# A decoder layer on one core: attention weights transposed by row halves, with four smaller moves of work around it

## The chip, the cores and the metric

One Trainium2 chip, one core of it. The metric is device microseconds of one execution of the whole program, as the median of several runs.

## The reference

Sixteen sequences of 128 tokens with 128 features go through one decoder layer, all in float32:

```python
x = layernorm(x + attention(x))            # 16 sequences, 16 heads of 64: Q, K, V, softmax(Q K^T / 8) V, then W_O
x = layernorm(x + cross(x, ctx_1024))      # 16 heads of 64; at each token, the heads attend to one another:
    scores = einsum('bshd,bsgd->bshg', q, k) / 8      # 16 x 16 for each token, softmax over g
    out    = einsum('bshg,bsgd->bshd', softmax(scores), v)   # then reshaped across tokens, then W_o
x = layernorm(x + ffn(x))                  # light: 128 -> 64 -> 128 for all tokens
                                           # heavy: 128 -> 512 -> 128 for the routed ones; 128 are chosen of 128
```

Both feed-forward parts therefore work on all tokens, with RMS normalisation ahead of them and a GELU inside.

## The kernel before

Five instruction streams are written by hand: TensorE (PE), VectorE (DVE), ScalarE (ACT), GpSimd (POOL) and SyncE (SP). They meet only through counting semaphores; nothing is scheduled by a planner, so the order of the code is the order on each engine. There are 16 sequences and 18 steps. Step s handles three sequences at once: the attention scores and softmax of sequence s, the attention output, first normalisation and cross queries of sequence s-1, and the cross output of sequence s-2. Projections of queries and keys are made for four sequences together, so the steps differ by phase, which is s modulo 4. A step of phase 3 projects the first queries of the next four, a step of phase 0 the rest of them, and a step of phase 1 the cross keys; the phase 2 step has none of that and is the shortest. On DVE, ACT, POOL and SP steps 3 to 14 are a loop of three rounds; PE's stream is written out.

PE's order in a step, with the lines of the kernel before: transposes of the second half of the attention weights of sequence s-1 (`transpose_p`, L1127), values (L1156 to L1158), weighted values (L1148), scores of heads 0 to 7 (L1223), output projection (L1168), a cross transpose (L1055), scores of heads 8 to 15 (L1223), cross values (L1162 to L1164), x1 transposed (L1308), cross weighted values (L1067), cross queries (`project_q2`, L1136), transposes of the first half of the weights of sequence s (L1127), cross output projection (`project_o2`, L1076), and cross scores (L1178). In phase 3 the first four query units (`project_qk`, L1028 to L1030) stand between the first half's transposes and L1076. In phase 0 the next units follow the second half's transposes, and they wait for DVE to have picked the cross scores (`pick_own`, L793 and L797).

A half is eight heads: a tile of 128 queries by 8 times 128 keys, which POOL divides by the row sums (L414). A transpose takes one head, 128 x 128, as the stationary operand, and the identity as the moving one:

```python
for i in range(4):
    hd = 4 * u + i
    last = nc.tensor.transpose(bank(T_BANK[u])[:, i * T:(i + 1) * T], p[:, hd * T:(hd + 1) * T], ident[:])
```

Four heads fill one PSUM bank, and ACT copies each bank out whole (`transposed`, L534). In the trace, a float32 product is two MATMUL records and two weight loads; a transpose is one of each. Products with 64 stationary rows or 64 columns are placed on parts of the array by their partitions: L1178, L1067 and L1223 use four parts of 64 x 64, L1136, L1148 and L1048 two parts of 64 columns.

DVE's work that matters here: `stats1` and `x1_out` make x1 (L769 to L779), `inverse_sums` the reciprocals that POOL waits for (L813), `values2_out` the cross values (L763), `q2_out` the cross queries out of PSUM in two units (L785), `regrouped` its half of the cross output (L699; ACT has the other, L499), and `attention_out` the attention output (L753). In steps of phase 3, `project_qk` writes its units 0 and 1 to the banks of the two units of `q2_out`, and its units 2 and 3 to the banks that ACT's and DVE's `regrouped` empty. `project_o2` waits for both halves of `regrouped` and the first unit of `q2_out`. POOL's `rstd1` makes the reciprocal deviation for x1 (L383, L385), waits for x1, and adds a bias to it (L389) before it divides the weights.

At the program's start, the query and key weights come in five parts, of which the first has 128 columns; ACT rounds each part (`split_hi`, L459), and DVE makes the rest (`split_lo`, L666). At the end of step 1, DVE scales the feed-forward weights (L915, L916), rounds them (L918) and subtracts (L920).

Of the kernel before, what the change touches and what calls it, by code (L numbers as in the profile page):

```python
# [50 lines left out]
def build(nc, x_nat, x_t, ctx_t, w_qk, w_v, w_o, b_qk, b_v, b_o,  # L51
# [10 lines left out]
    with ctx:  # L62
# [134 lines left out]

        def ot2_half(k2):

            return (ot2[:, k2 * K2 * 128:(k2 + 1) * K2 * 128].rearrange("p (k h e) -> p e k h", k=K2, h=H),  # L200
                    bank(PV2[k2]).rearrange("p (e k h) -> p e k h", k=K2, h=H))
# [80 lines left out]
        QK_PARTS = [slice(0, 128), slice(128, BANK)] + [slice(u * BANK, (u + 1) * BANK) for u in range(1, 4)]  # L282
# [66 lines left out]
        def _(pool):  # L349
# [31 lines left out]
            def rstd1(s, b_par):  # L381
                pool.wait_ge(mv1_ready, s)
                nc.gpsimd.tensor_tensor(ve1[:], mv1[:, 1:2], eps[:, 0:1], ALU.add).then_inc(ve1_ready, 1)  # L383
                pool.wait_ge(ve1_ready, s)
                nc.gpsimd.tensor_tensor(rs1[:], ve1[:], minus_half[:, 0:1], ALU.pow).then_inc(rs1_ready, 1)  # L385
                if isinstance(s, int) and s == 1:
                    pool.wait_ge(in_bo2, 16)
                pool.wait_ge(x1_ready, s)
                nc.gpsimd.tensor_tensor(x1b[b_par][:], x1[:], bo2_row[:], ALU.add).then_inc(x1b_ready, 1)  # L389

            def rms2(s):

                pool.wait_ge(ssm_ready, s - 1)
                nc.gpsimd.tensor_tensor(rn[:], ssm[:], minus_half[:, 0:1], ALU.pow).then_inc(rn_ready, 1)  # L394
                nc.gpsimd.tensor_tensor(x2b[:, bass.ds((s - 2) * D, D)], x2[:], bdl_row[:], ALU.add).then_inc(x2b_ready, 1)

            def step(s, h, g, phase, a, bc, d):
# [11 lines left out]
                for half in range(2):  # L409
                    if a:  # L410

                        pool.wait_ge(inv_ready, 2 * s + half + 1)
                        ph = p[:, half * 8 * T:(half + 1) * 8 * T].rearrange("q (h k) -> q h k", h=8)
                        nc.gpsimd.tensor_tensor(ph, ph, row_inv[:, 8 * half:8 * half + 8].unsqueeze(2).to_broadcast([T, 8, T]),  # L414
                                                ALU.mult).then_inc(p_ready, 1)
# [14 lines left out]
            rstd1(B, 1)  # L430
            minus_max2(LAST)
# [20 lines left out]
        def _(act):  # L452
# [170 lines left out]
            for u in (2, 3):  # L623
                act.wait_ge(mm_t, 4 * (B - 1) + u + 1)
                nc.scalar.activation(pt[:, u * BANK:(u + 1) * BANK], bank(T_BANK[u]), ACT.Copy).then_inc(pt_ready, 1)
# [33 lines left out]
        def _(dve):  # L659
# [140 lines left out]
            def step(s, h, g, phase, a, bc, d):  # L800
# [50 lines left out]
                if d:  # L851
                    if static and s == 2:
                        dve.wait_ge(in_mask, 16)
                    block_diagonal(s, 0)
                    block_diagonal(s, 1)
                if bc:
                    x1_out(s)
                if static and s == 0:
# [15 lines left out]
                if a:  # L874
                    inverse_sums(0)
                    score_max(2)
# [24 lines left out]
                if a:  # L901
# [10 lines left out]
                if static and s == 1:  # L912
# [4 lines left out]
                    dve.wait_ge(wup_scaled, 2)  # L917
                    nc.vector.tensor_copy(wup_hi[:], wup).then_inc(wup_split, 1)  # L918
# [100 lines left out]
        def _(pe):  # L1019
# [100 lines left out]
            def transpose_p(n, u):  # L1120

                if u % 2 == 0:

                    pe.wait_ge(p_ready, 2 * n + u // 2 + 1)
                for i in range(4):
                    hd = 4 * u + i
                    last = nc.tensor.transpose(bank(T_BANK[u])[:, i * T:(i + 1) * T], p[:, hd * T:(hd + 1) * T], ident[:])  # L1127
                last.then_inc(mm_t, 1)
# [53 lines left out]
            def step(s, h, g, phase, a, bc, d):  # L1182
# [45 lines left out]
                if static and s == 0:  # L1228
# [7 lines left out]
                    nc.tensor.matmul(bank(FIRST_BANKS[0]), wqk_hi[:, 0:128], xg_lo[:], start=False, stop=True).then_inc(mm_qk, 1)  # L1236
                    pe.wait_ge(w_lo, WQK_SPLIT[0])
                    project_qk(0, "A", lambda r: None, FIRST_BANKS, units=(1, 2, 3))
# [3 lines left out]
                if bc:  # L1242
                    transpose_p(s - 1, 2)
                    transpose_p(s - 1, 3)
# [96 lines left out]
                if a:  # L1341
# [4 lines left out]
                    transpose_p(s, 1)  # L1346
# [33 lines left out]
            transpose_p(B - 1, 2)  # L1380
            transpose_p(B - 1, 3)
# [149 lines left out]
```

## Time and profile before

| | |
|---|---|
| Time, median of 3 runs | 406.34 us (406.04 to 407.11) |
| The profiled execution's own time | 407.05 us, of which the span of the profile is 405.2 us |
| PE busy | 394.5 us, 97% of the span |
| DVE, ACT, POOL busy | 286.9, 240.5 and 146.7 us (71%, 59%, 36%) |
| PE's clock granted | 0.998 of full speed over the span |

The span runs from the first instruction to the last; 1.8 us of the execution lie outside it. A matmul's busy time counts its passage through the array, in which the next one has already begun, so the mean of one matmul is not what one more costs; what one more costs is seen in how far apart two groups begin.

### The profile page before, as it was taken

How to read it: one execution, taken by the hardware profiler on the slowest of the kernel's cores; microseconds unless marked ns; L12 is line 12 of the kernel's file. 1: busy time of each engine (PE TensorE's matmuls, PEld its weight loads, DVE VectorE, ACT ScalarE, POOL GpSimd, SP SyncE). 2: the span in 40 equal slices, each digit the busy share in tenths (PEclk: the TensorE clock that was granted, in tenths of full speed). 3: DMA queues.
4: the chain of work that ended last, by engine and by line, in shares of the span. 5: the costliest groups of instructions: out<-in, count | busy, mean ns of one | idle time of the engine just before them, and what ended most of it. 6: DMA issues, size and time to landing. Idle time of an engine off the chain costs nothing.

```text
span 405.2 us, 15945 instructions
## 1 busy us (share of the span) xinstructions
PE 394.5 (97%) x6580; PEld 343.2 (85%) x6580; DVE 286.9 (71%) x662; ACT 240.5 (59%) x814; POOL 146.7 (36%) x223
## 2 busy tenths in 40 slices
PE   8999999999999999999999999999999999999995
PEld 7797788788888888788888888888988888898985
DVE  4685786865758687866849678676848778687645
ACT  5685664745666584745567475645558566555552
POOL 0541444331523354331413454422415454323314
PEclk9999999999999999999999999999999999999999
DMA  7900112210110213110110213100101111211001
GB/s 244 371 27 8 43 25 63 65 37 2 33 31 11 46 29 91 37 28 8 32 25 15 49 29 92 34 21 8 42 15 24 41 39 23 47 39 26 27 28 52
DMA packets 43758, 19.33 MB, mean 48 GB/s; under 512 B 36592, under 2 KB 41200, under 8 KB 43696
## 3 DMA queue, kind: packets, MB, share of 16 engines
q1 hardware_dynamic: 42880, 16.88, 16.1%
q0 software_dynamic: 528, 1.45, 1.0%
q8 instruction: 52, 0.85, 0.8%
q10 hardware_dynamic: 288, 0.07, 0.1%
q14 instruction: 10, 0.08, 0.1%
HBM read 8.95 MB, written 1.05 MB: 25 GB/s over the span
## 4 chain that ended last, share of the span: by engine, by line
PE 85%; DVE 6%; SPq 3%; issue 2%; ACT 2%; DMA 1%; POOL 0%; POOLq 0%; DVEq 0%
PE ps L1223 7%; PE ps L1168 7%; PE ps L1048 7%; PE ps L1076 7%; PE ps L1148 7%; PE ps L1127 6%; PE ps L1136 6%; PE ps L1028 5%; PE ps L1030 4%; PE ps L1029 4%; PE ps L1178 4%; PE ps L1067 3%; SPq L317 3%; PE ps L1104 3%; PE ps L1162 2%; PE ps L1156 2%
## 5 line engine op out<-in xcount | busy, mean ns | idle before, releaser
L541 ACT ACTIVATE p<-ps,neg_max 128x128 f32<-128x128 f32 x256 | 90.3, 385 | 40.8 <-DVE neg_max L807 40.8
L414 POOL TENSOR_TENSOR p<-p,row_inv 128x1024 f32<-128x1024 f32 x32 | 60.7, 1898 | 60.2 <-DVE row_inv L813 60.2
L534 ACT ACTIVATE pt<-ps 128x512 f32<-128x512 f32 x62 | 34.3, 624 | 48.6 <-PE ps L1127 48.5
L541 ACT ACTIVATION_READ_ACCUMULATOR p<-ps,neg_max 128x1 f32 x256 | 57.9, 226 | 0.0
L807 DVE TENSOR_REDUCE neg_max<-ps 128x4 f32<-128x512 f32 x64 | 41.6, 673 | 4.8 <-PE ps L1223 4.0
L753 DVE TENSOR_TENSOR ot<-ps,bv 128x512 f32<-128x512 f32 x32 | 22.0, 689 | 27.6 <-PE ps L1148 27.5
L1136 PE MATMUL ps<-x1t,wq 128*64 128x64 f32 x1024 | 33.8, 224 | 1.6 <-DVE v2s L763 0.9
L1127 PE MATMUL ps<-ident,p 128*128 128x128 f32 x256 | 34.6, 279 | 0.8 <-POOL p L414 0.8
L1223 PE MATMUL ps<-kt,qt 64*64 64x128 f32 x1024 | 35.2, 275 | 0.0
L1136 PEld LDWEIGHTS ps<-x1t,wq 128*64 128x64 f32 x1024 | 31.5, 138 | 3.0 <-issue 1.9
L1168 PE MATMUL ps<-wo,ot 128*128 128x128 f32 x256 | 32.7, 281 | 0.6 <-DVE ot L753 0.6
L1168 PEld LDWEIGHTS ps<-wo,ot 128*128 128x128 f32 x256 | 29.9, 191 | 3.3 <-issue 3.2
L1148 PEld LDWEIGHTS ps<-pt,v 128*64 128x64 f32 x512 | 27.6, 137 | 5.8 <-issue 5.8
L1223 PEld LDWEIGHTS ps<-kt,qt 64*64 64x64 f32 x1024 | 27.6, 132 | 5.5 <-issue 5.3
L1076 PE MATMUL ps<-wo,ot 128*128 128x128 f32 x256 | 31.9, 278 | 0.0
L1076 PEld LDWEIGHTS ps<-wo,ot 128*128 128x128 f32 x256 | 30.0, 192 | 1.8 <-issue 0.2
L1148 PE MATMUL ps<-pt,v 128*64 128x128 f32 x512 | 31.5, 276 | 0.0
L1127 PEld LDWEIGHTS ps<-ident,p 128*128 128x128 f32 x256 | 27.6, 141 | 3.6 <-POOL p L414 0.9
L1048 PE MATMUL ps<-cg,wk 128*64 128x128 f32 x512 | 29.7, 274 | 0.0
L394 POOL TENSOR_TENSOR rn<-ssm,minus_half 128x1 f32<-128x1 f32 x16 | 8.8, 551 | 55.9 <-DVE ssm L744 55.9
L1048 PEld LDWEIGHTS ps<-cg,wk 128*64 128x64 f32 x512 | 27.8, 137 | 1.2 <-issue 1.0
L1028 PE MATMUL ps<-xg_hi,wqk_hi 128*128 128x512 f32 x63 | 26.2, 416 | 2.2 <-DVE qt L785 1.4
(152 smaller groups left out, 835.5 us busy)
## 6 DMA issues: line engine op xcount, KB each, us to landing
v<-v2s SPq DMA_DIRECT2D x256, 32.0 KB
xg<-x_t SPq DMA_DIRECT2D x4, 256.0 KB, 2.9
cg<-ctx_t SPq DMA_DIRECT2D x4, 256.0 KB, 3.4
wo<-w_o SPq DMA_DIRECT2D x2, 512.0 KB, 9.5
xres<-x_nat SPq DMA_DIRECT2D x15, 64.0 KB, 1.8
pt<-w_qk SPq DMA_DIRECT2D x3, 256.0 KB, 4.3
out<-x2b SPq DMA_DIRECT2D x3, 256.0 KB, 2.3
x2b<-w_v SPq DMA_DIRECT2D x1, 512.0 KB, 7.3
```

What stands on the lines that cost most here:

```text
L414: nc.gpsimd.tensor_tensor(ph, ph, row_inv[:, 8 * half:8 * half + 8].unsqueeze(2).to_broadcast([T, 8, T]), ALU.mult).then_inc(p_ready, 1)
L534: nc.scalar.activation(pt[:, u * BANK:(u + 1) * BANK], bank(T_BANK[u]), ACT.Copy).then_inc(pt_ready, 1)
L541: last = nc.scalar.activation(p[:, hd * T:(hd + 1) * T], bank(S_BANK[q])[:, pos * T:(pos + 1) * T], ACT.Exp, bias=neg_max[:, hd:hd + 1], a ...
L807: nc.vector.reduce_max(neg_max[:, first:first + 7:2], bank(S_BANK[q]).rearrange("p (h k) -> p h k", h=4), AX.X, negate=True).then_inc(max_ ...
L1028: nc.tensor.matmul(out_cols, w_hi_cols, m_hi, start=True, stop=False)
L1048: last = nc.tensor.matmul(bank(BLOCK_BANKS[blk][r])[64 * ih:64 * ih + 64, i * 128:(i + 1) * 128], wk2[:, hd * DH:(hd + 1) * DH], own, star ...
L1076: last = nc.tensor.matmul(bank(O2, D), ot2[:, k * 128:(k + 1) * 128], wo2[:, k * D:(k + 1) * D], start=k == 0, stop=k == K - 1)
L1127: last = nc.tensor.transpose(bank(T_BANK[u])[:, i * T:(i + 1) * T], p[:, hd * T:(hd + 1) * T], ident[:])
L1136: last = nc.tensor.matmul(bank(Q2[u])[64 * ih:64 * ih + 64, i * HALF:(i + 1) * HALF], wq2[:, hd * DH:(hd + 1) * DH], x1t[:, ih * HALF:(ih ...
L1148: last = nc.tensor.matmul(bank(PV_BANK[u])[64 * (i % 2):64 * (i % 2) + 64, (i // 2) * T:(i // 2 + 1) * T], v[b_par][:, hd * DH:(hd + 1) * ...
L1168: last = nc.tensor.matmul(bank(O, D), ot[:, c * T:(c + 1) * T], wo[:, c * D:(c + 1) * D], start=c == 0, stop=c == NC - 1)
L1223: mm = nc.tensor.matmul(bank(S_BANK[2 * half + i % 2])[qh * HALF:(qh + 1) * HALF, (i // 2) * T:(i // 2 + 1) * T], qt[rows, first:first + H ...
```

## The change

Five edits.

1. `transpose_p` takes a half of eight heads as 16 transposes of half a head each: 64 query rows by 128 keys as the stationary operand, a 64 x 64 piece of the identity as the moving one. The rows 0 to 63 of all eight heads fill one bank, the rows 64 to 127 another. ACT's copy scatters a bank in runs of 64 elements (`pt_part`).
2. POOL's `rstd1` loses the bias addition, which becomes `x1_biased`; POOL waits for x1, divides the first half of the weights, and only then adds the bias.
3. DVE's `regrouped` comes ahead of both units of `q2_out` in phases 0, 1 and 2, and behind both in phase 3 (it was between them). In step 1 the third maximum is taken before x1, and the second reciprocals between the two units of `q2_out`.
4. The rounding of the feed-forward weights moves from DVE at the end of step 1 to ACT in step 2, and the subtraction to the end of DVE's step 2.
5. The first two parts of the query and key weights become 256 and 256 columns (they were 128 and 384), and the third query unit waits for its own low part only before its last product.

```diff
+        def pt_part(u):
+            half, e = u // 2, u % 2
+            return (pt[:, half * 8 * T:(half + 1) * 8 * T].rearrange("p (h e q) -> p e h q", h=8, e=2)[:, e],
+                    bank(T_BANK[u]).rearrange("p (h q) -> p h q", h=8))
...
-        QK_PARTS = [slice(0, 128), slice(128, BANK)] + [slice(u * BANK, (u + 1) * BANK) for u in range(1, 4)]
+        QK_PARTS = [slice(0, 256), slice(256, BANK)] + [slice(u * BANK, (u + 1) * BANK) for u in range(1, 4)]
...
+            def x1_biased(s, b_par):
                 pool.wait_ge(x1_ready, s)
                 nc.gpsimd.tensor_tensor(x1b[b_par][:], x1[:], bo2_row[:], ALU.add).then_inc(x1b_ready, 1)
...
                 if bc:
                     rstd1(s, b_par)
+                    pool.wait_ge(x1_ready, s)
+                if a:
+                    over_sum(s, 0)
+                if bc:
+                    x1_biased(s, b_par)
+                if a:
+                    over_sum(s, 1)
...
-                    nc.scalar.activation(pt[:, u * BANK:(u + 1) * BANK], bank(T_BANK[u]), ACT.Copy).then_inc(pt_ready, 1)
+                    dst, src = pt_part(u)
+                    nc.scalar.activation(dst, src, ACT.Copy).then_inc(pt_ready, 1)
...
+                if static and s == 2:
+                    act.wait_ge(wup_scaled, 2)
+                    nc.scalar.activation(wup_hi[:], wup, ACT.Copy).then_inc(wup_split, 1)
...
+                    if d and phase < 3:
+                        regrouped(s)
                     q2_out(s, 0)
-                if d:
-                    regrouped(s)
-                if bc:
+                    if static and s == 1:
+                        inverse_sums(1)
                     q2_out(s, 1)
+                    if d and phase == 3:
+                        regrouped(s)
...
-                    dve.wait_ge(wup_scaled, 2)
-                    nc.vector.tensor_copy(wup_hi[:], wup).then_inc(wup_split, 1)
+                if static and s == 2:
                     dve.wait_ge(wup_split, 1)
                     nc.vector.tensor_tensor(wup_lo[:], wup, wup_hi[:].bitcast(fp32), ALU.subtract).then_inc(wup_split, 1)
...
+            def transpose_p(n, half):
+                pe.wait_ge(p_ready, 2 * n + half + 1)
+                for i in range(8):
+                    hd = 8 * half + i
+                    for e in range(2):
+                        rows = slice(HALF * e, HALF * e + HALF)
+                        mm = nc.tensor.transpose(bank(T_BANK[2 * half + e])[:, i * HALF:(i + 1) * HALF],
+                                                 p[rows, hd * T:(hd + 1) * T], ident[rows, rows])
+                        if i == 7:
+                            mm.then_inc(mm_t, 1)
```

How the instructions stand. On PE, around the first half's transposes in a step of phase 3, before:

```order
L1136 MATMUL ps<-x1t,wq2 64x64 x32
L1127 MATMUL ps<-ident,p 128x128 x8
L1028 MATMUL ps<-xg_hi,wqk_hi 128x512
L1029 MATMUL ps<-xg_lo,wqk_hi 128x512
L1030 MATMUL ps<-xg_hi,wqk_lo 128x512
```

and of the change at the same place:

```order
L1167 MATMUL ps<-x1t,wq2 64x64 x32
L1156 MATMUL ps<-ident,p 128x64 x16
L1056 MATMUL ps<-xg_hi,wqk_hi 128x512
L1057 MATMUL ps<-xg_lo,wqk_hi 128x512
L1058 MATMUL ps<-xg_hi,wqk_lo 128x512
```

Nothing changes its place on PE; eight transposes with 128 columns of output each became sixteen with 64. On DVE, in the same step, the rounded inputs' rest (`xg_lo`), the cross queries (`qt2`), the regrouping (`ot`) and the first evicted query unit (`qt`), before:

```order
L670 TENSOR_TENSOR xg_lo<-xg,xg_hi 128x512
L785 TENSOR_TENSOR qt2<-ps,bq2 128x64x8
L697 ISA
L699 COPY ot<-ps 128x8x64
L785 TENSOR_TENSOR qt2<-ps,bq2 128x64x8
L682 ISA
L683 TENSOR_SCALAR qt<-ps,bqk 128x512
```

and of the change:

```order
L692 TENSOR_TENSOR xg_lo<-xg,xg_hi 128x512
L807 TENSOR_TENSOR qt2<-ps,bq2 128x64x8 x2
L719 ISA
L721 COPY ot<-ps 128x8x64
L704 ISA
L705 TENSOR_SCALAR qt<-ps,bqk 128x512
```

The second unit of the cross queries has passed the regrouping. On POOL, in a looped step, from the deviation for x1 to the second half of the weights (`p`), before:

```order
L383 TENSOR_TENSOR ve1<-mv1,eps 128x1 [waits mv1_ready]
L385 TENSOR_TENSOR rs1<-ve1,minus_half 128x1 [waits ve1_ready]
L389 TENSOR_TENSOR x1b0<-x1,bo2_row 128x128 [waits x1_ready]
L412 ISA
L414 TENSOR_TENSOR p<-p,row_inv 128x1024 [waits inv_ready]
L412 REGISTER_ALU
L414 TENSOR_TENSOR p<-p,row_inv 128x1024 [waits inv_ready]
```

and of the change:

```order
L389 TENSOR_TENSOR ve1<-mv1,eps 128x1 [waits mv1_ready]
L391 TENSOR_TENSOR rs1<-ve1,minus_half 128x1 [waits ve1_ready]
L407 ISA [waits x1_ready]
L409 TENSOR_TENSOR p<-p,row_inv 128x1024 [waits inv_ready]
L397 TENSOR_TENSOR x1b0<-x1,bo2_row 128x128 [waits x1_ready]
L407 REGISTER_ALU
L409 TENSOR_TENSOR p<-p,row_inv 128x1024 [waits inv_ready]
```

The bias (`x1b0`) stands behind the first division; the wait for x1 stays ahead of it.

## Rows read from the trace of the kernel before

**Rows 1.** The page: span and instructions; engine, busy us, share, instructions.

```profile
span 405.2 us, 15945 instructions
PE 394.5 (97%) x6580; PEld 343.2 (85%) x6580; DVE 286.9 (71%) x662; ACT 240.5 (59%) x814; POOL 146.7 (36%) x223
```

**Rows 2.** The page: the chain that ended last, by engine.

```profile
PE 85%; DVE 6%; SPq 3%; issue 2%; ACT 2%; DMA 1%; POOL 0%; POOLq 0%; DVEq 0%
```

**Rows 3.** Groups by line: count, busy us, mean ns of one, idle before.

```profile
L1127 PEld LDWEIGHTS ps<-ident,p 128*128 128x128 f32 x256 | 27.6, 141 | 3.6 <-POOL p L414 0.9 <-issue 0.7
...
L1076 PEld LDWEIGHTS ps<-wo,ot 128*128 128x128 f32 x256 | 30.0, 192 | 1.8 <-issue 0.2
```

**Rows 4.** Timeline, PE, 130 to 137 us (phase 1 into 2): start, us.

```profile
132.12 1.09 PE L1127 MATMUL ps<-ident,p 128*128 128x128 f32 x8
133.15 2.02 PE L1076 MATMUL ps<-wo,ot 128*128 128x128 f32 x16
135.10 1.16 PE L1178 MATMUL ps<-kb,qt 64*64 64x64 f32 x64
136.19 1.09 PE L1127 MATMUL ps<-ident,p 128*128 128x128 f32 x8
137.04 0.48 PE L1156 MATMUL ps<-wv_hi,xg_lo 128*128 128x512 f32 x1
```

**Rows 5.** Timeline, weight loads, first two of a group: 149.7 and 150.7 us.

```profile
149.68 0.20 PEld L1127 LDWEIGHTS ps<-ident,p 128*128 128x128 f32 x2
...
150.68 0.30 PEld L1076 LDWEIGHTS ps<-wo,ot 128*128 128x128 f32 x2
```

**Rows 6.** Timeline, DVE and POOL, 131 to 134 us.

```profile
131.30 0.69 DVE L785 TENSOR_TENSOR qt<-ps,bq 128x512 f32<-128x512 f32 x1 [0.44 <-PE ps L1136]
131.91 1.09 DVE L699 COPY ot<-ps 128x512 f32<-128x512 f32 x1
...
133.70 1.90 POOL L414 TENSOR_TENSOR p<-p,row_inv 128x1024 f32<-128x1024 f32 x1 [2.91 <-DVE row_inv L813]
```

**Rows 7.** Timeline, DVE, a phase 3 step, at 169 us.

```profile
168.77 0.70 DVE L785 TENSOR_TENSOR qt<-ps,bq 128x512 f32<-128x512 f32 x1
```

**Rows 8.** Timeline, PE, the same step, 168 to 170 us.

```profile
168.41 0.40 PE L1029 MATMUL ps<-xg_lo,wqk_hi 128*128 128x512 f32 x1
168.65 0.39 PE L1030 MATMUL ps<-xg_hi,wqk_lo 128*128 128x512 f32 x1
169.52 0.50 PE L1028 MATMUL ps<-xg_hi,wqk_hi 128*128 128x512 f32 x1 [0.48 <-DVE qt L785]
```

**Rows 9.** Timeline, PE, phase 0 step, 176 to 177 us.

```profile
176.99 0.48 PE L1028 MATMUL ps<-xg_hi,wqk_hi 128*128 128x512 f32 x1
```

**Rows 10.** Timeline, DVE, the same step.

```profile
175.35 1.52 DVE L797 SCALAR_TENSOR_TENSOR s<-ps,own_j,s 128x256 f32<-128x256 f32 x3
```

**Rows 11.** Timeline, PE, steps 1 and 2, 45 to 52 us.

```profile
45.86 1.09 PE L1127 MATMUL ps<-ident,p 128*128 128x128 f32 x8 [0.76 <-POOL p L414]
...
51.84 0.91 PE L1168 MATMUL ps<-wo,ot 128*128 128x128 f32 x6 [0.56 <-DVE ot L753]
```

**Rows 12.** Timeline, DVE, the same stretch.

```profile
48.66 0.65 DVE L918 CAST wup_hi<-x2b 128x640 fp32r<-128x640 f32 x1
49.35 0.82 DVE L920 TENSOR_TENSOR wup_lo<-x2b,wup_hi 128x640 fp32r<-128x640 f32 x1
```

**Rows 13.** Timeline, PE, the start.

```profile
6.92 0.50 PE L1028 MATMUL ps<-xg_hi,wqk_hi 128*128 128x512 f32 x1 [0.76 <-DVE wqk_lo L666]
```

**Rows 14.** Timeline, PE, step 15, 346 to 349 us.

```profile
346.91 0.57 PE L1136 MATMUL ps<-x1t,wq 128*64 128x64 f32 x11 [0.69 <-issue]
...
348.33 0.83 PE L1076 MATMUL ps<-wo,ot 128*128 128x128 f32 x6
```

**Rows 15.** Groups by line: ACT's copies out of PSUM.

```profile
L534 ACT ACTIVATE pt<-ps 128x512 f32<-128x512 f32 x62 | 34.3, 624 | 48.6 <-PE ps L1127 48.5
...
L499 ACT ACTIVATE ot<-ps 128x512 f32<-128x512 f32 x16 | 18.1, 1134 | 1.0 <-PE ps L1067 1.0
```

More of the change, by code:

```diff
@@ L395, in rms2, with over_sum @@
                 nc.gpsimd.tensor_tensor(x2b[:, bass.ds((s - 2) * D, D)], x2[:], bdl_row[:], ALU.add).then_inc(x2b_ready, 1)
+            def over_sum(s, half):
+                pool.wait_ge(inv_ready, 2 * s + half + 1)
+                ph = p[:, half * 8 * T:(half + 1) * 8 * T].rearrange("q (h k) -> q h k", h=8)
+                nc.gpsimd.tensor_tensor(ph, ph, row_inv[:, 8 * half:8 * half + 8].unsqueeze(2).to_broadcast([T, 8, T]),
+                                        ALU.mult).then_inc(p_ready, 1)
             def step(s, h, g, phase, a, bc, d):
@@ L408, in step @@
                     rstd1(s, b_par)
[L409 to L415, printed above, removed]
+                    pool.wait_ge(x1_ready, s)
[5 more added lines that the diff above has]
+                    over_sum(s, 1)
                 if d:
@@ L430, in _ @@
             rstd1(B, 1)
+            x1_biased(B, 1)
             minus_max2(LAST)
@@ L624, in _ @@
                 act.wait_ge(mm_t, 4 * (B - 1) + u + 1)
-                nc.scalar.activation(pt[:, u * BANK:(u + 1) * BANK], bank(T_BANK[u]), ACT.Copy).then_inc(pt_ready, 1)
+                dst, src = pt_part(u)
+                nc.scalar.activation(dst, src, ACT.Copy).then_inc(pt_ready, 1)
             exp2(B)
@@ L854, in step @@
                     block_diagonal(s, 0)
+                if d:
                     block_diagonal(s, 1)
+                if static and s == 1:
+                    score_max(2)
                 if bc:
                     x1_out(s)
+                if a and bc:
+                    inverse_sums(0)
                 if static and s == 0:
@@ L873, in step @@
                     return
-                if a:
-                    inverse_sums(0)
+                if a and not (static and s == 1):
                     score_max(2)
@@ L891, in step @@
                         dve.wait_ge(in_own_j, 16)
+                    if d and phase < 3:
+                        regrouped(s)
                     q2_out(s, 0)
-                if d:
-                    regrouped(s)
-                if bc:
+                    if static and s == 1:
+                        inverse_sums(1)
                     q2_out(s, 1)
+                    if d and phase == 3:
+                        regrouped(s)
                 if phase == 0 and a and bc:
@@ L900, in step @@
                     qk_out(g + 1, "A")
-                if a:
+                if a and not (static and s == 1):
                     inverse_sums(1)
@@ L1118, in down_batch @@
                 last.then_inc(mm_y, 1)
[L1120 to L1128, printed above, removed]
+            def transpose_p(n, half):
[8 more added lines that the diff above has]
+                            mm.then_inc(mm_t, 1)
             def project_q2(s, u):
@@ L1236, in step @@
                     nc.tensor.matmul(bank(FIRST_BANKS[0]), wqk_hi[:, 0:128], xg_lo[:], start=False, stop=True).then_inc(mm_qk, 1)
+                    project_qk(0, "A", lambda r: None, FIRST_BANKS, units=(1,))
+                    pe.wait_ge(w_hi, 2)
+                    nc.tensor.matmul(bank(FIRST_BANKS[2]), wqk_hi[:, 256:384], xg_hi[:], start=True, stop=False)
+                    nc.tensor.matmul(bank(FIRST_BANKS[2]), wqk_hi[:, 256:384], xg_lo[:], start=False, stop=False)
                     pe.wait_ge(w_lo, WQK_SPLIT[0])
-                    project_qk(0, "A", lambda r: None, FIRST_BANKS, units=(1, 2, 3))
+                    nc.tensor.matmul(bank(FIRST_BANKS[2]), wqk_lo[:, 256:384], xg_hi[:], start=False, stop=True).then_inc(mm_qk, 1)
+                    project_qk(0, "A", lambda r: None, FIRST_BANKS, units=(3,))
                     pe.wait_ge(w_lo, WQK_SPLIT[1])
@@ L1242, in step @@
                 if bc:
-                    transpose_p(s - 1, 2)
-                    transpose_p(s - 1, 3)
+                    transpose_p(s - 1, 1)
                 if phase == 0 and a and bc:
@@ L1345, in step @@
                     transpose_p(s, 0)
-                    transpose_p(s, 1)
                 if phase == 3 and not static:
@@ L1378, in _ @@
                 step(s, s // 2, s // GB, s % GB, s < B, 1 <= s <= B, s >= 2)
-            transpose_p(B - 1, 2)
-            transpose_p(B - 1, 3)
+            transpose_p(B - 1, 1)
             pe.wait_ge(wup_split, 2)
```

## The prediction, made before the change was run

> **What bounds the kernel.** I read the page first: PE is busy for 394.5 of 405.2 us, the next engine for 71% [rows 1], and the chain of work that ended last runs over PE for 85% [rows 2]. So a microsecond less of PE work is a microsecond less of time, wherever no other engine is close behind. The second view is therefore PE's timeline over one step, where the reader sees groups that begin as the one before ends, without a bracketed wait [rows 4]. Then I looked, at each place that the change touches, for what ended last: DVE's and POOL's rows beside PE's.
>
> **The transposes.** What one costs is seen from how groups follow one another. Eight take 1.09 us from the first start to the last end, and the last lasts some 0.27; they begin about 0.11 apart. From the first transpose to the next group it is 1.03 us (132.12 to 133.15) where the cross output projection follows, and 0.85 (136.19 to 137.04) where the values follow [rows 4].
>
> No row shows a transpose of 64 rows. The nearest are the cross scores, products of 64 x 64 with 64 moving columns in four parts of the array: 64 records last 1.16 us, less some 0.22 for the last, so 16 sets of four begin 0.059 us apart. The next group begins 0.15 us behind the last of them, against 0.03 us where the values follow the transposes: that is what a change in the division of the array costs [rows 4]. A pair of new transposes covers the same array with the same 64 moving columns, but each loads 128 columns of weights. Can the load hide? Loading p takes less than loading wo, 141 against 192 ns [rows 3]. And at the start of a group, the first two loads of p begin 0.06 us apart (0.20 less 0.14), the first two of wo 0.11 (0.30 less 0.19) [rows 5]. A load of p thus occupies about 0.06 us, as long as the 64 columns stream. If the two halves of the rows load and stream side by side, as the four parts do, a pair costs 0.059 us.
>
> The Trainium skill states a rule that speaks against this (TensorE: Matmul & The Clock Gate, "LDWEIGHTS (loading the stationary operand)"): a load takes its columns divided by 1.2 ns, whatever its rows. By it each new load would take an estimated 107 ns, as much as a whole one, and there would be twice as many. The trace disagrees for loads of p [rows 5]; it agrees for wo.
>
> I take 0.059 us, being the row nearest in shape; the bounds are 0.055, which is as good as it, and 0.11, the price of an old transpose. A half then costs 8 x 0.059 + 0.15 = 0.62 us to the next group.
>
> **Where this is worth what.** (a) The first half in phases 0, 1 and 2 and in step 2, ten places: 1.03 - 0.62 = 0.41. But the projection behind it waits for DVE. Before, the regrouping ended at 133.00, just ahead of the projection's start at 133.15 [rows 4, 6]. The change puts it ahead of both units of cross queries. DVE stood idle for 0.44 us until the first unit at 131.30, so the regrouping can begin at 130.86 and end at 131.95, and the first unit, 0.69 long, at 132.64 [rows 6]. PE comes at 132.12 + 0.62 = 132.74: the wait is just met. I take 0.36 each: 3.6 us; the bounds are 0.41, and 0.15 if the projection should go on starting at 133.00.
> (b) The second half ahead of the values, or of the first feed-forward unit at the end, eight places: 0.85 - 0.62, less 0.03 as the next group starts in an array just redivided: 0.19 each, 1.5 us. The weights must be divided in time. POOL ended at 135.60 and PE came at 136.19 [rows 4, 6]; PE now comes 0.36 earlier, 0.2 us behind POOL, still without a wait.
> (c) The second half ahead of the cross keys (steps 5, 9, 13), where the next group has its own division of the array already: 0.38 each, 1.1 us.
> (d) The second half in steps 4, 8 and 12: the next unit waits for DVE's picked scores, which end at 176.87, and it began at 176.99 [rows 9, 10]. There is 0.1 us to be had at most: 0.3 us.
> (e) The first half in steps 3, 7 and 11: DVE gave the second unit of cross queries last, at 169.47, behind a regrouping of 1.1 us [rows 6, 7], and PE's second query unit stood until 169.52. The bracket says 0.48 us; a further 0.16 is lost since a record of 0.39 us is followed after some 0.24 when nothing waits [rows 8]. With the change the regrouping comes last, and the fourth unit, which needs it, is 1.4 us away: PE gets the 0.64. Of the shorter transposes it gets 0.08, as its first unit already followed the first cross queries closely. 0.72 each: 2.2 us.
> (f) Step 0: both halves stand together, and what follows waits for ACT's four copies; nothing.
> (g) Steps 1 and 2: the second half of step 1 waited 0.76 us for POOL [rows 11], as DVE made the reciprocals behind both units of cross queries. They now come between the two, a unit of 0.69 us [rows 6] earlier; I take 0.64. With 0.19 as in (b), PE is 0.83 ahead when DVE reaches the end of step 1. There the rounding and the subtraction, 0.65 and 0.82, go [rows 12], so that the attention output keeps up, and PE's wait of 0.56 on it [rows 11] goes too: 1.4 us together. The subtraction comes back at the end of DVE's step 2: between nothing, if DVE waits for PE there, and its 0.82; I charge 0.2, for DVE is busy 71% of its time. The rounding falls in ACT's step 2, where ACT's copies then wait for PE; nothing, and 0.65 without that cover.
> (h) The start: with 256 columns first, PE's second query unit needs no second part. Its wait of 0.76 us [rows 13] goes, and 0.16 as in (e); the first part is 64 KB longer and delays the inputs behind it, for which I leave off 0.1: 0.8 us. The bounds are 0.4 and 0.9.
> (i) Step 15 is of phase 3 but projects no queries, so the regrouping put last there is waited for by the output projection. By the rows the cross queries end at 346.91 + 0.57, the unit on DVE takes 0.65 and the regrouping 1.1, so the projection would begin at 349.2 and not at 348.33 [rows 6, 14]. But the 0.69 us ahead of 346.91 waited for no engine, and need not come again in that place; without it, it would be 0.2 late. I charge 0.45, and 0.2 for the last steps, where the second half's gain meets other waits.
> (j) POOL's division ahead of its bias: the first half is divided 0.4 us earlier, but PE asked for it more than 1 us later anyway; nothing. The bias is read a step later; nothing.
>
> **The sum.** 3.6 + 1.5 + 1.1 + 0.3 + 2.2 + 1.4 + 0.8 - 0.2 - 0.65 = 10.0 us. The profiled execution took 407.05 us, 1.85 of it outside the span, so it becomes 397.0. It lies 0.7 above the median of the runs shown; for the median I predict 396.3 us.
>
> **The rivals.** *No gain from the halves*: loads of 0.055 us come one behind the other, and a pair costs 0.11 us as an old transpose did. A half then costs 8 x 0.11 + 0.15 = 1.03. Then (a) and (c) give nothing, (b) loses 0.2 at eight places, (d) as much at three, (e) keeps 0.46 of its 0.72, (g) about 1.0, (h) 0.8, and 0.85 is charged as before: -1.6 - 0.6 + 1.4 + 1.0 + 0.8 - 0.85 = 0.15 us, which is no change, 406.2. For it: no row has a transpose on part of the array. Against: every product here that is split by rows overlaps, four parts in 0.059 us [rows 4]. I give 0.09.
> *Slower, by loads as long as wo's*: 0.11 us each, and one after the other. A half would cost 8 x 0.22 + 0.15 = 1.9 us, 0.9 to 1.05 more than now, at some 30 places: about 28 us, less 2 or 3 from the other edits, 432 us. It decides as soon as a pair costs more than 0.11 us, since at that price the other edits are used up. Against it stand the loads' starts [rows 5]. 0.05, with all that lies between. The skill's rule named above would lead here, if the two halves don't load side by side.
> *ACT's scattered copies*: ACT's other scattered copy takes 1134 ns where the plain one takes 624 [rows 15]. At that price the two copies of a half end 1 us later, the values that ACT copies behind them too, and the scores that wait for those, with DVE's sums; of 1 us I let 0.4 reach PE in each of 13 steps: 5 us of the 10 go, 401.3. Against it: the slow copy scatters single elements, the new one runs of 64. 0.05.
> The forecast's own case has the remaining 0.81: 393.5 to 399.5 us. At its low end pairs cost 0.055 us (1 us in all), nothing is charged under (i) and (a) has its 0.41; at its high end half of the places of (a) wait for DVE, and (g) and (h) bring half.
>
> **How the numbers follow.** A change of under 0.3% can't be told from none here: 405.1 to 407.6 us. Slower are the second rival and a quarter of the first, 0.07; the same is the rest of the first, 0.07; faster are the forecast's case and the third rival, 0.86. The range for 8 in 10 is 393.3 to 401.5: it takes in the third rival and leaves out the first two, 0.14, and the forecast's far ends.
>
> **What the profile will show.** Right: a half's 16 records begin in pairs 0.06 us apart, and the next group comes 0.6 us behind the first; in phase 3 no wait of the second query unit; no wait on POOL in step 2's first transposes. The means stay near 220 ns for one record. Wrong in the first rival's way: pairs 0.11 apart. Wrong in another: new waits in front of the cross output projection, on DVE's regrouping or cross queries, or ahead of the scores on ACT's values. What I trust least is DVE, whose rows follow PE's by 0.1 to 0.2 us in several places, so that a gain on PE there may turn into a wait.

## The result and the profile after

The change made the kernel 1.7% faster: 399.83 us, median of 4 runs (399.22 to 400.01), against 406.48 (406.04 to 407.11) in the same comparison; the ratio is 0.9833 (0.9815 to 0.985). The prediction was 396.3 us, with 393.3 to 401.5 as its range. The profiled execution took 399.96 us, 398.1 of it the span.

The page of the change, its busy times, the instruction queue of its part on DMA, and its chain, answer to [rows 1, 2]:

```profile
span 398.1 us, 16460 instructions
PE 386.8 (97%) x6836; PEld 335.9 (84%) x6836; DVE 286.6 (72%) x661; ACT 240.0 (60%) x815; POOL 146.8 (37%) x223
...
q8 instruction: 54, 0.88, 0.9%
...
PE 89%; DVE 3%; ACT 2%; DMA 2%; SPq 1%; issue 1%; POOL 1%; POOLq 0%; DVEq 0%
```

PE's share of the chain grew from 85% to 89%. The timeline of PE at the place of [rows 4] (start, length in us; in brackets the idle time before the group and what ended it):

```profile
126.97 1.96 PE L1167 MATMUL ps<-x1t,wq 128*64 128x64 f32 x59
129.22 0.39 PE L1167 MATMUL ps<-x1t,wq 128*64 128x64 f32 x5 [0.28 <-issue]
129.53 0.71 PE L1156 MATMUL ps<-ident,p 64*128 64x64 f32 x16
130.18 2.05 PE L1104 MATMUL ps<-wo,ot 128*128 128x128 f32 x16
132.16 1.16 PE L1209 MATMUL ps<-kb,qt 64*64 64x64 f32 x64
133.25 0.71 PE L1156 MATMUL ps<-ident,p 64*128 64x64 f32 x16
133.89 0.50 PE L1187 MATMUL ps<-wv_hi,xg_lo 128*128 128x512 f32 x1
```

A half of the transposes now lasts 0.65 us to the projection and 0.64 to the values, where it was 1.03 and 0.85: 0.38 and 0.21 gained. The two loads and the two products of a pair begin 3 to 4 ns apart, and the pairs follow each other after 0.062 us, where 0.059 was forecast. This is what the Trainium skill says of products on different rows of the array (TensorE: Matmul & The Clock Gate, "Why this matters for your kernels"): they start at most 4 ns apart and run together. The rule on loads from the same page of the Trainium skill, which the prediction weighed, does not set the pace here: a pair of loads follows the one before after 0.062 us, and by the rule one load alone would take an estimated 0.107. But the first lines show something else: inside the cross queries, ahead of the transposes, PE stopped for no engine ("issue"). This is where a part of the gain went. DVE, at the place of [rows 6], has the order that was forecast:

```profile
127.65 1.09 DVE L721 COPY ot<-ps 128x512 f32<-128x512 f32 x1
128.58 0.69 DVE L807 TENSOR_TENSOR qt<-ps,bq 128x512 f32<-128x512 f32 x1
129.64 0.69 DVE L807 TENSOR_TENSOR qt<-ps,bq 128x512 f32<-128x512 f32 x1 [0.38 <-PE ps L1167]
```

Phase 3, answering to [rows 8]: the second query unit, L1056 at 165.64, follows without a wait, and stands 3.88 us earlier than before, where the record at 165.17 stands 3.24 earlier. The 0.64 are there.

```profile
163.88 0.71 PE L1156 MATMUL ps<-ident,p 64*128 64x64 f32 x16
164.94 0.39 PE L1056 MATMUL ps<-xg_hi,wqk_hi 128*128 128x512 f32 x1 [0.36 <-issue]
165.17 0.40 PE L1057 MATMUL ps<-xg_lo,wqk_hi 128*128 128x512 f32 x1
165.41 0.40 PE L1058 MATMUL ps<-xg_hi,wqk_lo 128*128 128x512 f32 x1
165.64 0.39 PE L1056 MATMUL ps<-xg_hi,wqk_hi 128*128 128x512 f32 x1
```

The start, answering to [rows 13]. The first line is of the 12 products on zeros that PE runs until the inputs come, the second of the first real product, the last of the third block of query units. Before, and then of the change:

```profile
1.07 4.40 PE L1024 MATMUL ps<-warm 128*128 128x128 f32 x24 [1.07 <-DVE warm L660]
5.22 0.48 PE L1232 MATMUL ps<-xg_hi,wqk_hi 128*128 128x512 f32 x1
...
12.08 0.47 PE L1028 MATMUL ps<-xg_hi,wqk_hi 128*128 128x512 f32 x1
```

```profile
1.07 5.19 PE L1052 MATMUL ps<-warm 128*128 128x128 f32 x24 [1.07 <-DVE warm L682]
6.02 0.48 PE L1263 MATMUL ps<-xg_hi,wqk_hi 128*128 128x512 f32 x1
...
12.22 0.47 PE L1056 MATMUL ps<-xg_hi,wqk_hi 128*128 128x512 f32 x1 [0.36 <-DVE qt L705]
```

The wait of 0.76 us is gone, but PE began at 6.02 us and not at 5.22, and the third block came 0.14 later, behind a wait for DVE. Step 15, answering to [rows 14], PE and then DVE:

```profile
339.57 0.79 PE L1156 MATMUL ps<-ident,p 64*128 64x64 f32 x16
341.87 2.02 PE L1104 MATMUL ps<-wo,ot 128*128 128x128 f32 x16 [1.51 <-DVE ot L721]
```

```profile
338.85 0.69 DVE L770 TENSOR_TENSOR xg_lo<-xnt,xg_hi 128x512 fp32r<-128x512 f32 x1 [0.53 <-ACT xg_hi L538]
339.45 1.28 DVE L807 TENSOR_TENSOR qt<-ps,bq 128x512 f32<-128x512 f32 x2
340.65 1.07 DVE L721 COPY ot<-ps 128x512 f32<-128x512 f32 x1
```

Steps 1 and 2, answering to [rows 11]: of the 0.76 us of waiting for POOL 0.26 are left, and the wait for DVE at the output projection is gone.

```profile
45.38 0.71 PE L1156 MATMUL ps<-ident,p 64*128 64x64 f32 x16 [0.26 <-POOL p L409]
...
50.54 2.05 PE L1199 MATMUL ps<-wo,ot 128*128 128x128 f32 x16
```

ACT's copies, answering to [rows 15]: the scatter costs nothing, 614 ns a copy after 624.

```profile
L552 ACT ACTIVATE pt<-ps 128x512 f32<-128x512 f32 x62 | 34.0, 614 | 46.6 <-PE ps L1156 46.3
```

**Two theories of the stops.** PE's idle time on "issue" was 0.9 us in two places before (0.69 of it in [rows 14]); it is 1.6 us in four places now, and three more stops are hidden in the modelled length of a group, as at 146.56 us, where 16 transposes last 1.01 us and not 0.71. (The second place of before: the last four products of L1178, at 367.38 us.) Count all of PE's rows in the trace (loads, products, semaphore events) in the order of their starts: the two stops of before come at rows 11968 and 12736, those of the change at 4288, 5056, 5824, 7616, 8384, 9152 and 11712. Each is 192 more than a multiple of 256. A round of four steps has 3340 rows, 12 more than 13 blocks of 256, so a boundary between blocks falls at nearly the same place of the program in each round, as 4288 and 7616 do. The queue of instruction fetches has 54 packets of 16 KB, about one for 256 rows of PE. So the first theory is that PE's instructions come in blocks of 256, and PE stops when it has used up a block before the next has come; the change puts 512 more rows, 256 of them products, into shorter time, and so meets this more often. The Trainium skill has a sentence on it (Advanced Engine Details and Errata, "ISA Cache"): a line of the instruction cache is 16 KB or 256 instructions, and there are two lines, though it gives 128 KB for TensorE, which would be eight. The spacing agrees; how many lines there are no run here shows. The rival is that the stops belong to the place, such as the switch of the array's division at the transposes.

### The profile page after: what moved, and what is told of

Read it like the earlier page. It is cut to its first block, busy times and chain, and to the rows that moved or that the text cites. A ratio compares the mean times of both kernels' runs of the same rounds, so it can differ in the third digit from the quotient of the medians.

```text
span 398.1 us, 16460 instructions
## 1 busy us (share of the span) xinstructions
PE 386.8 (97%) x6836; PEld 335.9 (84%) x6836; DVE 286.6 (72%) x661; ACT 240.0 (60%) x815; POOL 146.8 (37%) x223
## 3 DMA queue, kind: packets, MB, share of 16 engines
q0 software_dynamic: 528, 1.45, 1.0%
HBM read 8.95 MB, written 1.05 MB: 25 GB/s over the span
## 4 chain that ended last, share of the span: by engine, by line
PE 89%; DVE 3%; ACT 2%; DMA 2%; SPq 1%; issue 1%; POOL 1%; POOLq 0%; DVEq 0%
PE ps L1254 8%; PE ps L1104 8%; PE ps L1199 7%; PE ps L1076 7%; PE ps L1167 7%; PE ps L1179 7%; PE ps L1056 5%; PE ps L1156 5%; PE ps L1058 4%; PE ps L1057 4%; PE ps L1095 4%; PE ps L1209 4%; PE ps L1132 3%; PE ps L1193 2%; PE ps L1187 2%; PE ps L1195 2%
## 5 line engine op out<-in xcount | busy, mean ns | idle before, releaser
L1056 PE MATMUL ps<-xg_hi,wqk_hi 128*128 128x512 f32 x62 | 25.4, 409 | 0.8 <-DVE qt L705 0.4
L1057 PE MATMUL ps<-xg_lo,wqk_hi 128*128 128x512 f32 x62 | 24.5, 395 | 0.0
L1058 PE MATMUL ps<-xg_hi,wqk_lo 128*128 128x512 f32 x62 | 24.5, 395 | 0.0
```

Source lines behind the costliest of these rows:

```text
L1056: nc.tensor.matmul(out_cols, w_hi_cols, m_hi, start=True, stop=False)
L1057: nc.tensor.matmul(out_cols, w_hi_cols, m_lo, start=False, stop=False)
L1058: return nc.tensor.matmul(out_cols, w_lo_cols, m_hi, start=False, stop=True)
```

## The experiments

All in five rounds; times are medians in us (lowest to highest), ratios are to the kernel before on the same chip, with 95% intervals.

| run | us | ratio |
|---|---|---|
| pad96 | 397.43 (397.27 to 397.93) | 0.9776 (0.9761 to 0.9791) |
| pad8 | 399.68 (398.2 to 401.69) | 0.9841 (0.9813 to 0.9868) |
| start_old | 400.19 (399.47 to 401.33) | 0.985 (0.9827 to 0.9872) |
| halves_alone | 404.57 (403.66 to 408.65) | 0.9959 (0.9939 to 0.9979) |
| before_pad40 | 407.67 (407.09 to 408.1) | 1.0035 (1.0023 to 1.0046) |
| full_pad40 | 403.45 (402.97 to 404.0) | 0.9931 (0.9917 to 0.9944) |
| pad96_step15 | 396.6 (395.74 to 398.04) | 0.9767 (0.9747 to 0.9787) |
| pad96_start | 396.94 (396.48 to 397.38) | 0.9772 (0.9759 to 0.9786) |
| pad96_regroup | 402.86 (402.42 to 403.93) | 0.9897 (0.9866 to 0.9929) |
| pad96_wup | 398.48 (398.02 to 399.06) | 0.9786 (0.9756 to 0.9817) |
| pad96_pool | 396.89 (396.52 to 398.8) | 0.9756 (0.9723 to 0.9789) |
| best | 397.21 (396.28 to 399.23) | 0.9764 (0.973 to 0.9798) |

**pad96: PE's rows 96 places later.**

```diff
-WARM_PRODUCTS = 12
+WARM_PRODUCTS = 36
...
-                nc.tensor.matmul(bank(O, D), warm[:], warm[:], start=True, stop=True)
+                nc.tensor.matmul(bank(O, D)[0:32, 0:44], warm[:, 0:32], warm[:, 0:44], start=True, stop=True)
```

> The changed kernel with the 12 products ahead of its first input (128 x 128 each) replaced by 36 of 32 x 44, which fill about the same time: PE's records stand 96 places later in its instruction stream and nothing else changes. Theory of fetched instructions: PE's stream comes in blocks of 256 records, and the stops inside the cross queries and the first half's transposes (0.5, 0.3, 0.6, 0.6, 0.2, 0.2 us at 128.8, 146.8, 216.6, 234.5, 322.0 and 252.7 us of the changed kernel) stand where a block begins whose predecessor was consumed faster than the next could be fetched; 96 places on, block boundaries fall into stretches where 256 records take longer, and the stops go: 397.7 us (2.1 less than the 399.83 of the change). Rival, that the stops belong to the place in the program (the switch of the array's division, a semaphore): they stay, 399.8 us.

It took 397.43 us, 2.4 less than the change, and varied by 0.7 us only. PE's list of waits has no "issue" left. The stretch where the change stopped at 129.22, now:

```profile
127.11 2.08 PE L1167 MATMUL ps<-x1t,wq 128*64 128x64 f32 x64
129.13 0.71 PE L1156 MATMUL ps<-ident,p 64*128 64x64 f32 x16
129.77 0.49 PE L1104 MATMUL ps<-wo,ot 128*128 128x128 f32 x2
```

Same place, no stop: the rival falls. Group by group, PE gets ahead of the change by 0.1 to 0.65 us at seven places, 2.8 us in all, and nowhere else by more than 0.1.

**pad8: 8 places later.** The same edit with 14 products of 110 columns.

> The changed kernel with 14 products ahead of its first input in place of 12, each a little narrower: PE's records stand 8 places later. Theory of fetched instructions: the stops stay near where they were but each stands exactly 8 records earlier in the program, and is somewhat shorter, since the block that ends there holds fewer of the dense records: about 0.6 us less than the change in all, 399.2 us. Rival, that the stops belong to the place in the program: same places, 399.8 us.

It took 399.68 us, but its runs lie between 398.2 and 401.69, so the 0.6 us can't be read. The place can. The stop at row 11712, of start_old (below), whose rows stand as in the change, and then of pad8:

```profile
319.19 1.96 PE L1167 MATMUL ps<-x1t,wq 128*64 128x64 f32 x58
321.68 0.45 PE L1167 MATMUL ps<-x1t,wq 128*64 128x64 f32 x6 [0.53 <-issue]
```

```profile
317.84 1.84 PE L1167 MATMUL ps<-x1t,wq 128*64 128x64 f32 x54
320.29 0.56 PE L1167 MATMUL ps<-x1t,wq 128*64 128x64 f32 x10 [0.60 <-issue]
```

It stands behind 54 products and not 58: four products with their loads, 8 rows, earlier. In pad8's profiled execution no other block stopped for over 0.15 us. So whether a tight block stops, and for how long, differs between executions; that would explain why the times of pad8 scatter, but only one of its executions has a trace.

**start_old: edit 5 undone.** `QK_PARTS` with 128 and 384 columns, and `project_qk(0, "A", ..., units=(1, 2, 3))` behind one wait, as before.

> The changed kernel with edit 5 undone (parts of 128 and 384 columns, the third query unit in its old form). Theory from the trace of the change: the longer first part delays PE's first product from 5.22 to 6.11 us, and PE stands 0.24 us later at the third block of units than before, so undoing the edit gives 0.24 us back: 399.6 us. The prediction's step (h): the edit is worth 0.8 us, so undoing it costs them: 400.6 us.

400.19 us, which lies between the two, and the stops' scatter hides the difference. The trace: the third block began at 11.85 us, but the first real product at 6.03, as in the change (the rows of the change give 6.02 and 0.14, not the 6.11 and 0.24 named above). So the longer first part of the weights had not delayed the first product; I had that wrong. pad96_start, below, settles the price.

**halves_alone: edit 1 alone, on the kernel before.** `transpose_p`, its calls and `pt_part` as in the change.

> The kernel before with edit 1 alone (row halves and the scattered copies). By the prediction's terms, with the regrouping still between the two units of cross queries: (a) 10 x 0.15, (b) 1.5, (c) 1.1, (d) 0.3, (e) 3 x 0.08, (g) 0.2, together 4.8 us, less 1.0 for the stops at fetched blocks, which the denser stream adds: 402.7 us. Rival, that the projection does not wait for the regrouping in its old place and (a) has its full 10 x 0.36: 400.6 us. Rival, that edit 1 brings nothing by itself: 406.5 us.

404.57 us: 2 us less than before, where 3.8 were expected. It has six stops of its own of 0.3 to 0.7 us at rows 192 above a multiple of 256. In the trace, the projection behind the first half starts no earlier than before in an undisturbed step, since it waits for DVE:

```profile
PE ps L1084 <- DVE ot L707: 2.4, 6, 0.9
PE ps L1036 <- DVE qt L793: 1.4, 3, 0.6
```

(Columns: who waits for whom; us in total, times, longest.) The halves alone bring (b) and (c), and nothing of (a).

**before_pad40: the kernel before, 40 places later** (22 products of 64 x 72 ahead of the inputs).

> The kernel before with the 12 products ahead of its first input replaced by 22 smaller ones, so that PE's records stand 40 places later and the block boundaries fall into stretches where 256 records take over 4 us. Theory of fetched instructions: the two stops of the kernel before (0.9 us at 346.0 and 0.4 at 367.0, less the usual distance) go as well, 1.2 us: 405.4 us. Rival: the kernel before has no such cost and stays at 406.6 us.

407.67 us, slower by 0.35%: a miss. The two stops did go. The one at 367 us gives 0.5, but of the 0.95 at step 15 only 0.17 stays, since the projection then waits 0.78 for the regrouping. And two stops came, again 192 more than a multiple of 256 (rows 5568 and 7360), 0.5 us each, the first of them hidden by the wait of the second query unit; the 22 products ended late, so that PE's first real one came at 6.54 us and the third block at 12.63, 0.55 later. Against the profiled execution of before, 407.05 us, this explains the 0.4 us that its own has more; of the 1.45 between the medians some is left unexplained. My rule for tight blocks, 256 rows in under 4 us, was too simple: these two blocks took 4.2 us without their stops, and their fetch began 2.6 and 3 us behind the block ahead of it, where it is mostly about 0.6.

**full_pad40: edit 1 undone in the change**, with the same 22 products.

> The changed kernel with edit 1 undone (full transposes and plain copies), and 22 small products ahead of the first input, as in before_pad40, so that no stop falls in. Against pad96, which has the halves and no stops (397.43 us), the terms of the prediction that the halves bring are gone: (a) 3.6, (b) 1.5, (c) 1.1, (d) 0.3, of (e) 0.24, of (g) 0.2: 6.9 us more, 404.3 us. Rival, that the earlier regrouping alone keeps part of (a): 403 us or less.

403.45 us, with one stop of 0.9 us. The edits without the halves thus bring 2.8 us against the kernel before, and 4.2 against before_pad40, which has the same padding and stops of its own; the trace shows 0.74 of it at each second query unit. The earlier regrouping by itself lets the projection start 0.10 us earlier at each of the ten places, and the cross scores behind it 0.17. The halves on top bring the projection 0.29, of which 0.10 are lost again at the cross scores.

**pad96_step15: regrouping first in step 15 too.**

```diff
-                    if d and phase < 3:
+                    if d and (phase < 3 or static):
                         regrouped(s)
...
-                    if d and phase == 3:
+                    if d and phase == 3 and not static:
                         regrouped(s)
```

> pad96 with the regrouping of step 15 placed ahead of both units of cross queries, as in the phases 0 to 2, instead of behind them. Theory: the output projection of that step waits 1.37 us longer than before for the regrouping, and with the regrouping first it comes as in the other steps: 1.2 us less than pad96, 396.2 us. Rival: the cross queries come 1.1 us later on DVE and the cross scores wait for them, so that 0.4 us or less is left: 397.0 us.

396.6 us, between the two. In the trace the projection comes 0.74 us earlier; it now waits 0.85 us for the first cross queries (L807), which DVE takes up late because L770, for the feed-forward part, stands ahead of them.

**pad96_start: edit 5 undone in pad96.**

> pad96 with edit 5 undone (parts of 128 and 384 columns). Theory from the traces: the third block of units begins at 12.32 and 12.35 us with 256 columns first, at 12.08, 12.02 and 11.85 with 128 first, since the last part of the weights is split later: undoing gives 0.3 us: 397.1 us. The prediction's step (h), the edit being worth 0.8 us: 398.2 us.

0.9772 against 0.9776 for pad96: no difference. In the profiled executions of this study the third block begins at 11.82, 11.84, 11.85, 11.98, 12.08 and 12.63 us with 128 columns first, and at 11.79, 11.92, 12.22, 12.23, 12.27, 12.36, 12.50 and 12.62 with 256. (Of the starts named in the expectation, 12.32, 12.35 and 12.02 are not among them.) Edit 5 is worth nothing, or 0.3 us in the wrong direction.

**pad96_regroup: the regrouping between the units of cross queries again** (`q2_out`, `regrouped`, `q2_out` in every phase).

> pad96 with the regrouping between the two units of cross queries again in all phases (that part of edit 3 undone). Theory from the run of edit 1 alone, where the output projection starts no earlier in an undisturbed step: all ten places of (a) lose 0.36, (e) loses 0.64 three times, and step 15 gets 0.6 back, since its regrouping comes earlier: 397.43 + 3.6 + 1.9 - 0.6 = 402.3 us. By the prediction's bound for (a), 0.15 of 0.36 kept, it would be 400.8 us.

402.86 us: the first theory. PE comes 0.39 us later at each of the ten projections, and 0.83 at each second query unit with its next record; step 15 gets 0.6 back.

```profile
131.32 0.91 PE L1102 MATMUL ps<-wo,ot 128*128 128x128 f32 x6 [0.32 <-DVE ot L721]
```

**pad96_wup: edit 4 undone.** The rounding and the subtraction stand at the end of DVE's step 1 again.

> pad96 with edit 4 undone (rounding and subtraction of the feed-forward weights on DVE at the end of step 1). By the traces, the attention output of step 2 comes 0.63 us later again and step 3 gets 0.33 us back: 397.43 + 0.30 = 397.7 us. By the prediction, 0.56 less 0.2: 397.8 us. Rival, that DVE's work there is hidden anyway: 397.4 us.

398.48 us, 1.05 more than pad96 where 0.3 was expected; the intervals of the ratios overlap, but the trace shows it: the attention output in step 2 comes 1.33 us later, and 0.33 come back in step 3. In pad96 PE is ahead by more than the 0.56 us of [rows 11], so the same work on DVE makes it wait longer.

**pad96_pool: edit 2 undone.** `x1_biased` ahead of both `over_sum`.

> pad96 with edit 2 undone (POOL adds the bias ahead of the first division). The prediction's step (j), nothing: 397.4 us. Rival, that with the shorter transposes PE now comes soon enough for the 0.4 us on POOL to count at the ten steps' first halves: up to 401 us.

396.89 us, not to be told from pad96. From the third block of query units on no group moves against pad96 by more than 0.1 us.

**best: pad96 with edit 5 undone, step 15's regrouping first, and L770 behind the cross queries there.**

> pad96 with edit 5 undone and with step 15's regrouping first, and the subtraction for the first feed-forward inputs in step 15 moved behind the cross queries, where nothing waits for it yet. From the runs: 397.43 - 0.49 for the start, - 0.83 for the regrouping, and - 0.85 for the wait of the output projection on the cross queries that was left there: 395.3 us. Rival, that the subtraction is late for the first feed-forward unit in its new place and gives half of its gain back: 395.7 us.

397.21 us, a miss. The profiled execution, the fastest (396.28), shows where it went. At step 15 the projection comes 1.66 us earlier than in pad96; 0.39, 0.47 and 0.17 us are given back to three waits behind it:

```profile
340.58 0.71 PE L1156 MATMUL ps<-ident,p 64*128 64x64 f32 x16 [0.32 <-POOL p L409]
351.18 0.30 PE L1428 MATMUL ps<-perm,x 128*128 128x128 f32 x1 [0.31 <-DVE x L801]
351.77 0.41 PE L1095 MATMUL ps<-pt,v 64*64 64x64 f32 x13 [0.30 <-DMA v<-v2s]
```

So pad96 is shown to beat the change: its interval, 0.9761 to 0.9791, lies below the change's 0.9815 to 0.985. Neither pad96_step15 nor best can be told from pad96.

## Why the prediction was right, and where its size was off

The direction, the mechanism and the pair's price (0.059 us forecast, 0.062 measured) were right. That the time lies in the range is in part luck: 399.83 us is beyond 399.5, the far end of the forecast's own case, and inside only because the range takes in the third rival, slow scattered copies, which did not come. By the profiled executions 10.0 us were forecast and 7.1 came. Set against pad96, where no stop is in the way, the terms from the third block of query units on make 10.0 us where 9.2 were forecast. Term by term, by the starts of the groups in pad96 and in the kernel before:

- (a) 0.36 forecast, 0.39 measured, at ten places, of which 0.03 is lost again up to the next group: right. The lower bound was wrong: without the regrouping ahead not 0.15 but nothing is left (halves_alone, pad96_regroup). Edits 1 and 3 pay together: each alone gives the projection 0 and 0.10 us.
- (b) 0.19 forecast, 0.21 measured, of which 0.02 is lost again; (c) 0.38 and 0.38. (e) 0.72 forecast and 0.84 to 0.86 measured, since the record behind the second unit's first gains another 0.10; (d) 0.1 and 0.02 to 0.05.
- (g) 1.4 forecast from the start to step 2; in the change's own trace the output projection there went from 51.84 to 50.54 us, though the third block came 0.14 later: 1.44. Of POOL's wait 0.26 stayed, where none was forecast. The subtraction at the end of step 2 costs 0.33, not 0.2.
- (h) is the first step that failed: 0.8 forecast, nothing measured (pad96_start). The wait of 0.76 us in [rows 13] was real in that execution, because PE's products on zeros ended early and the first real one came at 5.22 us. In the change they lasted until 6.02, by which time the weights were split and there was nothing to wait for; nor was there with the old parts and a first product at 5.96 (halves_alone). In the profiled executions with 12 products of 128 columns that first product came at 5.22, 5.96, 6.02 and 6.03 us, as TensorE's clock rose at different times (last section). And where PE did begin early with the new parts, the gain was lost again. In pad96 the first real product came at 5.42 us and the second query unit waited for nothing, but then the third block waited 0.77 us for DVE, whose evictions stood behind the last part of the weights; in pad96_pool, begun at 5.36, it waited 0.57. So I priced a wait from one execution, in a stretch that differs between executions, and did not look for the next wait behind it. PE and then DVE, of pad96:

```profile
6.43 0.40 PE L1056 MATMUL ps<-xg_hi,wqk_hi 128*128 128x512 f32 x1
...
12.27 0.47 PE L1056 MATMUL ps<-xg_hi,wqk_hi 128*128 128x512 f32 x1 [0.77 <-DVE qt L705]
```

```profile
10.77 0.69 DVE L688 TENSOR_TENSOR wqk_lo<-pt,wqk_hi 128x512 fp32r<-128x512 f32 x1 [1.19 <-ACT wqk_hi L476]
11.38 1.40 DVE L705 TENSOR_SCALAR qt<-ps,bqk 128x512 f32<-128x512 f32 x2
```

- (i) a cost of 0.45 forecast for step 15, 0.42 measured, as 1.37 for the projection, which then waits, less 0.95 for the vanished stop; 0.6 of this is the regrouping put last (pad96_regroup). That they agree is luck: 0.45 was half of the 0.9 that the rows gave, chosen between that and 0.2. The second stop, at 367 us, went too and gave 0.5, which no term had; the 0.2 charged for the last steps was not seen.
- (j) nothing, and nothing measured (pad96_pool). The scattered copies, a rival, cost nothing either.

What the sum didn't have at all is the supply of PE's instructions: 2.8 us of new stops in the profiled execution. The step that failed is the second sentence of the prediction, that a microsecond less of PE work is a microsecond less of time unless another engine is near. Here no other engine was near, and PE stood still for its own instructions. The split halves PE's time for a transpose but doubles its instructions, and a denser stream meets the fetch. The trace of before held the sign: in (i) I read the 0.69 us on "issue" as a chance of the place that need not return. It hung on the count of rows, 11968, which lies 192 above a multiple of 256.

So −10.0 + 0.8 + 0.14 for the start, + 2.8 for the stops, − 0.5 − 0.2 for what went better, leave −7.0; measured −7.1. Two small slips in the working: 0.85 − 0.62 − 0.03 is 0.20 and not 0.19, and the three terms of the own case's low end make 394.2 us and not 393.5.

What stays open: what sets the start of a fetch. It began mostly some 0.6 us behind the first row of the block ahead, but in some blocks up to 2.3 us before it and in others up to 3.7 behind it (4.8 in the first block). Several of the late ones begin in the attention scores just ahead of the long products of the cross values. Nor was a version tried that makes the stream sparser, with fewer rows and no padding.

## What to carry to other kernels

A split that saves array time by more and smaller instructions must also be priced in instructions: look for stops that wait on no engine, count PE's rows up to them, and if they stand at one remainder of a block, shift the stream by a few dozen instructions and time again before judging an edit. An edit that shortens the work ahead of a wait and one that moves up what is waited for may each be worth nothing alone. A wait at the program's start should be read from several executions.

## What the runs showed of the hardware

Over the 14 profiled executions, every gap of more than 0.28 us within a group of short products stood within one row of 192 more than a multiple of 256. Taking the packets of the instruction queue in order, one for each block, no block's first row came sooner than 2.2 us after its fetch had begun. At 19 of the 22 stops of over 0.3 us PE went on 2.2 to 2.8 us after that begin; at the other three, all at row 5824, 3.3 us after it. The packet itself took 0.88 to 1.60 us.

The products on zeros run at two paces, a record each 0.21 us and later each 0.11, and the faster one began at 4.2 us before and at 5.9 in the change, PE having run such products since 1.07 us in both. The trace's first record of the granted clock, 1.00, which is the level of 2.4 GHz, begins at 4.15 and 5.82 us, so the pace doubled as that clock was granted. What was granted until then no record says, though the views print 1.00 there too; half the pace would be the level of 1.2 GHz. In the 14 executions the first record begins at 4.01 to 7.11 us. In eleven the pace doubled within 0.1 us of it; in the other three it begins at 6.88 us or later, behind the last product on zeros, and the pace did not change.
